# Ternary weights prepared inside the last steps of the channel attention instead of in a stage of their own

## The reference

```python
# layer 0, attention over channels: per batch, heads of 16 of the rows
qk = einsum('bdm,bdn->bmn', qh, kh) * scale
ret = einsum('bmn,bcn->bcm', softmax(qk), vh)        # added to x
# layer 0, feed-forward part with ternary weights (layernorm ahead of it)
def weight_quant(w):
    scale = clip(mean(abs(w)), 1e-5, None)           # one scale for a whole tensor
    return clip(round(w / scale), -1, 1) * scale
def hbitlinear(x, w, bits):                          # fwht: Walsh-Hadamard transform
    return einsum('bsh,oh->bso', act_quant(fwht(x), bits), weight_quant(w))
h = square(relu(hbitlinear(x, w_up, 8)))             # w_up 1024 x 512
out = hbitlinear(h, w_down, 8)                       # w_down 512 x 1024
# layer 1: causal attention with 16 heads, then a workspace feed-forward part
```

## Time and profile before

| What | us |
|---|---|
| median of 3 runs (3947.9 to 3956.12) | 3953.05 |
| the profiled execution, whole time | 3952.62 |
| its span in the trace | 3950.6 |
| last issue of a store of `attention0` | 1582.85 |
| first instruction of `prepare_ffn` | 1586.39 |
| first instruction of `ternary_ffn` behind it | 1618.96 |
| first multiplication by reciprocals (L649) | 1631.03 |
| first instruction of `causal_attention` | 2279.19 |

### The profile page before, as it was taken

One profiled execution on the slowest core, in us unless ns is written; L12 is line 12 of the kernel. 1 busy time (PEld: TensorE's weight loads), 2 busy tenths in 40 slices (PEclk: granted clock), 3 DMA queues, 4 the chain that ended last, 5 costly groups with the idle time before them and its releaser, 6 DMA issues. The chain is left out here.

```text
span 3950.6 us, 86378 instructions
## 1 busy us (share of the span) xinstructions
PE 3598.4 (91%) x24451; PEld 1799.6 (46%) x24451; DVE 2844.3 (72%) x4477; ACT 2574.0 (65%) x6419; POOL 1623.4 (41%) x2090
## 2 busy tenths in 40 slices
PE   5999999999999999299999979999995899999997
PEld 1222222222222222277777734444443655666664
DVE  5888888888888886477777767777775456464555
ACT  2777777777777777277777657777774454545454
POOL 6444444444444441466666422222222134242524
PEclk9999999999999999699999999999997999999999
DMA  7777777777777773333333223333233012030302
GB/s 115 120 124 120 123 125 122 121 124 119 123 125 123 121 118 57 110 112 110 113 115 111 74 89 92 95 96 90 91 96 128 34 56 74 18 113 2 129 1 75
DMA packets 342550, 385.80 MB, mean 98 GB/s; under 512 B 58433, under 2 KB 223041, under 8 KB 342337
## 3 DMA queue, kind: packets, MB, share of 16 engines
q1 hardware_dynamic: 315712, 348.69, 40.8%
q10 hardware_dynamic: 26624, 34.63, 3.4%
HBM read 196.52 MB, written 84.93 MB: 71 GB/s over the span
## 5 line engine op out<-in xcount | busy, mean ns | idle before, releaser
L302 DVE TENSOR_REDUCE a_neg_max<-a_max_ps 128x2 f32<-128x1024 f32 x1024 | 1200.9, 1219 | 197.7 <-PE a_max_ps L354 174.0
L380 ACT ACTIVATE a_P<-a_ring_ps 128x512 f32<-128x512 f32 x2048 | 1084.2, 602 | 382.3 <-PE a_ring_ps L336 378.9
L354 PE MATMUL a_max_ps<-a_K,a_Q 96*128 96x512 bf16 x2048 | 621.5, 385 | 43.9 <-DMA a_K<-a_k_split 39.9
L336 PE MATMUL a_ring_ps<-a_Q,a_K 98*128 98x512 bf16 x2048 | 618.0, 383 | 6.5 <-DMA a_Q<-a_max_rows 4.4
L365 PE MATMUL a_pv_ps<-a_P,a_V 128*32 128x512 f32 x4096 | 544.9, 604 | 1.8 <-ACT a_out_sb L385 1.8
L336 PEld LDWEIGHTS a_ring_ps<-a_Q,a_K 98*128 98x128 bf16 x2048 | 159.0, 96 | 660.9 <-ACT a_P L380 586.2
L1163 ACT ACTIVATE c_P<-c_s_ps,c_bias 128x128 f32<-128x128 f32 x1024 | 362.2, 368 | 137.9 <-DVE c_bias L1035 129.0
L1092 PE MATMUL c_s_ps<-c_KD,c_qT 128*128 128x512 f32 x512 | 276.7, 622 | 33.4 <-ACT c_qT L1154 28.9
L1031 DVE TENSOR_REDUCE c_neg_max<-c_s_ps 128x4 f32<-128x512 f32 x256 | 175.4, 685 | 163.6 <-PE c_s_ps L1093 163.6
L354 PEld LDWEIGHTS a_max_ps<-a_K,a_Q 96*128 96x128 bf16 x2048 | 183.3, 98 | 220.5 <-issue 42.9
L256 POOL TENSOR_SCALAR a_var_eps<-a_mean_var 128x1 f32<-128x1 f32 x64 | 12.3, 192 | 645.8 <-DVE a_mean_var L318 645.5
(11 more groups left out here) (250 smaller groups left out, 7085.4 us busy)
## 6 DMA issues: line engine op xcount, KB each, us to landing
a_Q<-a_q_split SPq DMA_DIRECT2D x384, 128.0 KB
a_K<-a_k_split SPq DMA_DIRECT2D x384, 128.0 KB
heads_out<-a_out_sb ACTq DMA_DIRECT2D x128, 256.0 KB, 2.1
a_x_in<-in_x_dram SPq DMA_DIRECT2D x64, 256.0 KB, 3.6
a_c_in<-in_ctx_dram SPq DMA_DIRECT2D x64, 256.0 KB
a_cT_in<-in_ctxT_dram SPq DMA_DIRECT2D x64, 256.0 KB
b_x_in<-in_x_dram SPq DMA_DIRECT2D x64, 256.0 KB, 2.7
b_o_in<-heads_out SPq DMA_DIRECT2D x64, 256.0 KB
```

What stands on the lines that cost most here:

```text
L302: dve.tensor_reduce(neg_max[:, p, 2 * u:2 * u + 2], max_ps[u % 2][:, :, :], AX.X, ALU.max, negate=True).then_inc(max_taken, 1)
L336: pe.matmul(ring(s, use_of(k))[:, :], K[i][:, h, n:n + 128], Q[i][:, h, :], start=True, stop=True).then_inc(scores_filled, 1)
L354: last = pe.matmul(max_ps[u % 2][:, j, :], Q[i][0:KROW, h, m:m + 128], K[i][0:KROW, h, :], start=True, stop=True)
L380: act.activation(P[p][k // NT][:, k % NT, :], ring(s, use_of(k))[:, :], ACT.Exp, scale=SCALE).then_inc(exp_done, 1)
```

## The change

`prepare_ffn` is gone. A new object `FfnState`, made ahead of `attention0`, holds what both stages use: the ternary weights, coefficients, identity, Hadamard matrix, sums and reciprocals with their semaphores, which are cleared behind `ternary_ffn`. `attention0` now does the following. At its start it loads the Hadamard matrix beside the identity, and DVE prepares both and a matrix of ones. At SP's k = 117 four chunks of 512 KB (all of `w_up`) go into four buffers `w_in`, and the sums of batches 0 to 3 are loaded. Behind its maxima of steps 118 to 125 DVE sums the absolute values of one chunk, and in steps 119 to 121 also makes one reciprocal. SP reloads a buffer when its chunk has been summed. Each chunk is loaded twice, once for the sum and once for the rounding. PE makes the product with the ones in its step 126, behind the seventh score. DVE then rounds, clips and converts eight chunks; ACT has no part in it. The later stages are as they were, but for `ternary_ffn`, whose SP queue now begins with the rows.

```diff
 # attention0, SP
+            def load_weights(j):
+                c = j % 4
+                src = ffn.up_rows[:, c:c + 1, :] if j % 8 < 4 else ffn.down_rows[:, 2 * c:2 * c + 2, :]
+                sp.dma_start(w_in[:, c, :].rearrange("p (k n) -> p k n", k=src.shape[1]), src).then_inc(w_loaded[c], 16)
             def step(s):
+                if 119 <= s.k:
+                    sp.wait_ge(w_sums_done, s.k - 118)
+                    load_weights(s.k - 115)
+                if s.k == 117:
+                    for j in range(4):
+                        load_weights(j)
+                    for p in range(2):
+                        sp.wait_ge(out_stored[p], 16 * 4)
+                    for b in range(4):
+                        sp.dma_start(ffn.sums[:, b, :], ffn.rows[b, :, 16, :].rearrange("h (p m) -> h p m", m=32)).then_inc(ffn.sums_loaded[b], 16)
                 if s.half(8) == 0 and s.exists(8):
...
             run_steps(sp, -8, 2, 116, 126, step)
+            for b in range(FIRST):
+                sp.wait_ge(ffn.recip_done, b + 1)
+                sp.dma_start(ffn.recips[b], ffn.recip[:, b, :]).then_inc(ffn.recips_stored[b], 16)
+            for j in range(12, 16):
+                sp.wait_ge(w_ternary_done, j - 11)
+                load_weights(j)
 # attention0, POOL, behind its steps
+            pool.wait_ge(w_scale_done, 1)
+            pool.tensor_tensor(w_root[:, :], w_scale[:, 1:2], w_half[:, :], ALU.pow).then_inc(w_root_done, 1)
 # attention0, DVE
-            dve.wait_ge(ident_loaded, 16)
+            dve.wait_ge(ident_loaded, 32)
             dve.tensor_copy(identb[:, :], identf[:, :]).then_inc(ident_ready, 1)
+            dve.tensor_copy(had[:, 128:256], had[:, 0:128]).then_inc(ident_ready, 1)
+            dve.tensor_scalar(had[:, 256:384], had[:, 0:128], -1.0, None, ALU.mult).then_inc(ident_ready, 1)
+            dve.memset(w_ones[:, :], 1.0).then_inc(ident_ready, 1)
...
+                if 118 <= s.k:
+                    j = s.k - 118
+                    dve.wait_ge(w_loaded[j % 4], j // 4 * 16 + 16)
+                    dve.tensor_reduce(w_sums[:, j // 4, j % 4:j % 4 + 1], w_in[:, j % 4, :], AX.X, ALU.add,
+                                      apply_absolute_value=True).then_inc(w_sums_done, 1)
+                if 119 <= s.k < 119 + FIRST:
+                    b = s.k - 119
+                    dve.wait_ge(ffn.sums_loaded[b], 16)
+                    dve.reciprocal(ffn.recip[:, b, :], ffn.sums[:, b, :]).then_inc(ffn.recip_done, 1)
             run_steps(dve, -7, 1, 115, 125, step)
+            dve.wait_ge(w_total_filled, 1)
...
+            for j in range(8):
+                i, c = j // 4, j % 4
+                dst = ffn.up[:, c, :] if i == 0 else ffn.down[:, 2 * c:2 * c + 2, :].rearrange("p k n -> p (k n)")
+                dve.wait_ge(w_loaded[c], i * 16 + 48)
+                dve.tensor_scalar(w_in[:, c, :], w_in[:, c, :], w_inv[:, i:i + 1], ROUND, ALU.mult, ALU.add).then_inc(w_rounded, 1)
+                dve.wait_ge(w_rounded, j + 1)
+                dve.tensor_scalar(w_in[:, c, :], w_in[:, c, :], ROUND - 1.0, ROUND + 1.0, ALU.max, ALU.min).then_inc(w_clipped, 1)
+                dve.wait_ge(w_clipped, j + 1)
+                dve.tensor_scalar(dst, w_in[:, c, :], ROUND, None, ALU.subtract).then_inc(w_ternary_done, 1)
...
 # attention0, PE
+                    if s.k == 126 and k == 6:
+                        pe.wait_ge(w_sums_done, 8)
+                        pe.wait_ge(max_taken, GROUPS * 2 * G)
+                        pe.matmul(max_ps[0][:, 0, 0:8], w_ones[:, :], w_sums[:, :, :].rearrange("p i j -> p (i j)"),
+                                  start=True, stop=True).then_inc(w_total_filled, 1)
 # decoder
-    attention0(nc, x, ctx, ctxT, ident, heads_out)
-    ternary_ffn(nc, x, heads_out, recips, hadamard, ident, w_upT, w_downT, x2)
+    with ExitStack() as st:
+        ffn = FfnState(nc, st, w_upT, w_downT, heads_out, recips, hadamard)
+        attention0(nc, x, ctx, ctxT, ident, heads_out, ffn)
+        ternary_ffn(nc, x, ffn, x2)
```

More of the change, by code:

```diff
@@ L98, in run_steps, with __init__, sb, attention0 @@
         body(Step(0, k))
-def attention0(nc, x, ctx, ctxT, ident, heads_out):
+ROUND = 1.5 * 2.0 ** 23
+class FfnState:
+    def __init__(self, nc, st, w_upT, w_downT, heads_out, recips, hadamard):
+        def sb(name, shape, dt):
+            return st.enter_context(nc.sbuf_tensor("w_" + name, shape, dt))
+        sem = Semaphores(nc, "w_", st)
+        KU, KD = w_upT.shape[0] // 128, w_downT.shape[0] // 128
+        NU, ND = w_upT.shape[1], w_downT.shape[1]
+        assert KU * NU == KD * ND
+        self.N = KU * NU
+        self.up_rows = w_upT.rearrange("(k p) n -> p k n", p=128)
+        self.down_rows = w_downT.rearrange("(k p) n -> p k n", p=128)
+        self.C1, self.RI = float(KU * 128) ** -0.5, float(KD * 128) ** -0.5
+        self.rows = heads_out.rearrange("(b g) (j r) m -> b (g j) r m", g=2, r=32)
+        self.recips, self.hadamard = recips, hadamard
+        self.up, self.down = sb("up_ternary", [128, KU, NU], BF16), sb("down_ternary", [128, KD, ND], BF16)
+        self.coef = sb("coef", [128, 2], F32)
+        self.identf, self.identb = sb("identf", [128, 128], F32), sb("identb", [128, 128], BF16)
+        self.had = sb("had", [128, 384], F32)
+        self.sums, self.recip = sb("sums", [128, 4, 32], F32), sb("recip", [128, 4, 32], F32)
+        self.sums_loaded, self.recips_stored = ([sem(f"{n}{i}") for i in range(4)] for n in ("sums_loaded", "recips_stored"))
+        self.recip_done = sem("recip_done")
+def attention0(nc, x, ctx, ctxT, ident, heads_out, ffn):
     B, C, M = x.shape
@@ L526, in ternary_ffn @@
     EPS = 1e-5
-    rows = heads_out.rearrange("(b g) (j r) m -> b (g j) r m", g=2, r=32)
+    rows, recips = ffn.rows, ffn.recips
+    identf, identb, had = ffn.identf, ffn.identb, ffn.had
+    sums, recip = ffn.sums, ffn.recip
+    sums_loaded, recips_stored, recip_done = ffn.sums_loaded, ffn.recips_stored, ffn.recip_done
     with ExitStack() as st:
-        up, down, coef = prepare_ffn(nc, st, w_upT, w_downT)
         def sb(name, shape, dt):
@@ L602, in _ @@
             first = At(0, 0, B)
-            for b in range(4):
-                load_sums(first, -b)
-            sp.dma_start(identf[:, :], ident).then_inc(const_in, 16)
-            sp.dma_start(had[:, 0:128], hadamard).then_inc(const_in, 16)
-            for b in range(3):
-                store_recips(first, -b)
             for b in range(2):
@@ L681, in invert_sums @@
                 dve.reciprocal(recip[:, i, :], sums[:, i, :]).then_inc(recip_done, 1)
-            for b in range(3):
-                invert_sums(At(0, 0, B), -b)
-            dve.wait_ge(const_in, 32)
-            dve.tensor_copy(identb[:, :], identf[:, :]).then_inc(const_ready, 1)
-            dve.tensor_copy(had[:, 128:256], had[:, 0:128]).then_inc(const_ready, 1)
-            dve.tensor_scalar(had[:, 256:384], had[:, 0:128], -1.0, None, ALU.mult).then_inc(const_ready, 1)
             def step(t):
```

120 lines of the change are left out of this document (36 added, 84 removed).

## The result

| | before | after |
|---|---|---|
| median of the runs | 3953.05 (3947.9 to 3956.12) | 3929.84 (3928.73 to 3934.05) |
| span of the profiled execution | 3950.6 | 3926.6 |
| first instruction behind `attention0`'s block | 1586.39 | 1586.11 |
| first multiplication by reciprocals | 1631.03 | 1593.21 |
| first `b_relu` on ACT | 1656.53 | 1618.79 |

The ratio is 0.9949 with a 95% interval of 0.9939 to 0.9959: clearly faster, by 23 us, where 34 were forecast. The table already tells where to look. Up to the first `b_relu` the changed kernel is 37.74 us ahead, at the next stage's first instruction only 24.00. The stages behind keep these 24.0. So 13.7 us were lost inside the FFN's pipeline, whose code the change leaves as it was.

A forecast was written before the change was run, and what follows sets the result against it. PE was taken to bound attention, then a serial chain of `prepare_ffn` and the FFN's start. The terms -32.6 - 5.2 + 3.4 + 0.3 + 0 + 0 + 0.5 = -33.6 us from 3952.62 gave 3919.0 us, range 3914 to 3930.

The forecast's parts named there:

- Part 1: `prepare_ffn` stage goes and the FFN's block starts where that stage started: -32.6 us.
- part 2: FFN's start: SP begins with the rows instead of issuing them behind sums, constants and stores: -5.2 us.
- Part 3: Sums and reciprocals between DVE's maxima in attention, a lag of 1.5 us free, the excess charged per step: +3.4 us.
- rival A: DVE in attention falls behind and pays each sum in full, +9.1 instead of +3.4: 3924.7 us; chance 0.14.
- C: Attention's DVE lags are all absorbed, -3.4: 3915.6 us; chance 0.07.
- Part 4: Product with ones on PE, ahead of the eighth score of step 126: +0.3 us (0 to 0.6).
- Part 5: Rounding on DVE's free end of attention, done 1577.7 to 1582 with at least 4 us of cover, reloads hidden: 0.
- rival E: Conversion is serial, each chunk waiting for its reload, 52 us late: 3971 us; chance 0.03.
- Part 6: SP's queue and DMA in attention: added loads and later copies of batches 62 and 63 fit: 0 (-0.8 to +4).
- Part 7: Edges: `FfnState` semaphores cleared behind the FFN, +0.5 us (0 to 0.9); extra constants at the start cost 0.
- Rival D: At the start, constants miss the gaps between POOL's memsets, POOL's chain starts 0.6 later: 3919.6; forecast including D has 0.60.
- B: DMA loads and shifted copies delay maxima rows or Q and K, +5 us: 3924; chance 0.10.

The follow-up runs named there:

- 12 memsets: Changed kernel plus 12 tiny memsets on DVE behind its conversions, so the FFN's loop begins at 582: 3910.06 us, ratio 0.9893.
- before, 10 memsets: Kernel before plus 10 tiny memsets on DVE at the start of `prepare_ffn`, so the FFN's loop begins at 560: 3958.09 us, ratio 1.0015 to before.
- 8 memsets: Changed kernel plus 8 tiny memsets on DVE behind its conversions, so the FFN's loop begins at 578: 3939.27 us, ratio 0.9973.
- with 10: Changed kernel plus 10 tiny memsets on DVE behind its conversions, so the FFN's loop begins at 580: 3910.89 us, ratio 0.99.
- doubled sums: Changed kernel with each of the eight sums taken twice and 4 tiny memsets, FFN's loop at 582: 3920.68 us.

## Why the prediction was wrong

It gave 3919.0 us with a range of 3914 to 3930; the time was 3929.84, inside the range by 0.2 and beside every case that made it. The direction and the mechanisms of its seven parts were right in the main; one cost of 13.7 us was missing.

**The step that failed is the sum itself**: "Sum: -32.6 - 5.2 + 3.4 + 0.3 + 0 + 0 + 0.5 = -33.6 us". It goes from the end of the attention straight to the end of the program. It has no term for the FFN's loop, taken to run as before because none of its code changed. It ran 13.7 us longer (636.40 against 622.66). Shown: the position of the loop in DVE's program decides this. The old kernel moved to 570 loses 9.8 us, the changed one moved to 551 or 580 is back at 619.67 and 621.75, and the instruction packets go with it. The difference in DVE's instructions could have been counted before the run. The old profile pointed at the place, though not at the cost: five waits of 0.4 us for "issue" at the very instruction behind the jump.

How a wait of 3 us becomes a loss can be read downstream. PE's waits between 1700 and 2140 us in the changed kernel:

```profile
PE b_qT_ps L828 <- DVE b_q1T L751: 10.9, 5, 2.4
```

Five waits, one for each jump, up to 2.4 us. They aren't among PE's in the kernel with 12 memsets. And POOL's, in the changed kernel:

```profile
POOL b_var_eps L662 <- DVE b_mean_var L733: 19.3, 15, 2.5
```

with 12 memsets:

```profile
POOL b_var_eps L665 <- DVE b_mean_var L736: 0.8, 4, 0.3
```

Of some 3.0 + 0.8 us waited at each jump the pipeline lost 2.7 (13.7 / 5). With one wait of 3.0 (before, 10 memsets) it lost 0.9: 4.3 / 5. With 8 memsets the five waits are 31.7 us, 6.3 each, and the FFN is 7.0 a jump longer than with 10: (656.90 - 621.75) / 5. That profiled execution was 9 us above its kernel's median, so the 7.0 is its own and not typical. A short wait is in part absorbed by what the engines have ahead; of a long one little is.

By its own parts:

**Part 1 and part 2, right.** The stage is gone (-32.57), and the first multiplication comes 7.10 us behind the block's start instead of 12.07: -4.97 where -5.2 was forecast. The reciprocals' part was tested alone: 4.43 us of queue and 11.29 to the multiplication. The multiplication is 37.82 us earlier in all (1631.03 - 1593.21), which looks like the forecast's -37.8 and is chance: the two parts gave 37.54, parts 3 and 4 took 1.40 of it, where 3.7 was forecast, and 1.68 came from the attention ahead of the change, whose step 118 began earlier (1471.90 against 1473.58), for which the forecast has no term. So the FFN's first row was issued at 1586.11 and not near 1590.

**Part 3, right in its rule, too large in its sum.** +3.4 was forecast. From the CAST of step 118 to the last one are 83.62 us before (1473.58 to 1557.20) and 85.26 after (1471.90 to 1557.16), +1.64. The free lag of 1.5 us was right. The changed kernel and the one with doubled sums have twelve steps in which the first maxima come more than 1.6 us behind the CAST (1.69 to 3.96), and in all twelve the period above 11.76 is that lag less 1.5 to 1.6. Step 119 of the doubled sums has 3.96 and a period of 14.13. So rival A (each in full) falls as a rule, and C (all absorbed) too. What was too large is two things. Step 120 was charged a stretched CAST of 0.59; it took 0.30 and the step cost 0.36, not 0.85. And the steps before the change were not all 11.76: they were 1.3 us above it together, most of it in one of 12.69, which is 11.92 now, and the 0.8 us of the earlier trace rows is in no list after. Above 11.76 the steps of the changed kernel are 2.9 us, near the forecast, but 1.3 of that was there already.

**Part 4, nothing** instead of +0.3: from the last CAST to the next block are 29.19 us before and 28.95 after.

**Part 5, right.** DVE's last conversion ended at 1578.35. The third operation, whose price was bounded by 0.62 and 1.15, takes 0.69 for 1024 columns, the same as the second; a chunk takes 2.12 us. No conversion waited for a reload, so rival E had nothing.

**Part 6, right.** SP's copies of batch 62 went at 1487.26 instead of 1483.43, 3.8 later and not 5, those of 63 followed, and no wait of PE was put down to them.

**Part 7, right.** From the last `b_relu` to the next block are 24.54 us before and 24.94 after, +0.4 where +0.5 was said. POOL's first operation on the moments is at 13.41 instead of 13.38. Rival D's lost gap did not happen; DVE's constants were done by 5.1. The hold that the section describes is there once more: the CAST began at 3.15 instead of 2.56 and ended at 4.47 again, and a copy beside it at 4.55, both right behind POOL's memset (0.89 + 3.51). So this trace agrees with the section that rival D quotes. Only the time that rival D drew from it was wrong: the TENSOR_SCALAR went at 4.46, in the gap.

Rivals A, B and F happen to lie near 3924 and widened the range to 3930. That it held the time is owed to their sizes, not to their mechanisms: none of the three is in the trace.

The clock was as expected, 0.52 of full speed between 1593.20 and 1619.00 us, so the lower level.

Without the loop's loss the change gives 3910, not 3919. Of the 9 us between them 2 are part 3, 0.5 part 4, 1.2 a shorter attention ahead of the change (the CAST at 1460.65 instead of 1461.82), 3.2 the FFN (2.7 shorter, 619.92 against 622.66, where +0.5 was forecast) and 1.7 the two stages behind (1671.4 us from `causal_attention`'s first instruction to the end before, 1669.7 with 12 memsets). What makes the last three is not tested; the FFN of the kernels without the wait lies between 619.67 and 622.66.

## What to carry to other kernels

A change has a side that its diff does not show: it moves every instruction behind it on the same engine. Where a loop on an engine is longer than one piece of its program (254 to 262 instructions here), count where it begins before and after. The count alone did not place the workspace loop, so look in the profile too: for waits for "issue" at its first instruction, one for each jump back, and for the packets of the instruction queue in that stretch. A wait hidden behind another engine's work, as in the workspace loop, costs nothing and is in no list. If they grew, a few harmless instructions in an idle place, or a few fewer, are worth more than much of the work on the change: here 12 memsets brought 20 us, where the change itself had brought 23.

## What the hardware showed unexpectedly

The cost of such a loop depends on how many of its instructions lie ahead of the edge. With 20 it is one wait of 3.1 us, the fetch of the first piece, and the next piece is there in time. With 9 or 10 it is 3.1 and 0.8, or 3.1 and up to 1.7. With 2 it is up to 7.0, two fetches behind each other. With none it is 0.5. The packet times above show that these are fetches. The rule of the Trainium skill cited above agrees with the edge, with the length of a piece, and with the jump as the place: between 578 and 580 the time falls by 28 us. It says also that crossing a boundary is mostly hidden where no jump intervenes. Waits of 0.4 to 0.5 us at the jump in the kernels that fit, and none elsewhere in the loop, agree with that too.

Memsets of one column cost DVE next to nothing: twelve of them are one row of 0.19 us in the profile.
